# Last graph convolution: weights applied before the aggregation, adjacency blocks as TensorE's stationary operand

## What is computed

```python
def _gcn_conv(x, W, b, src, dst, norm, n_nodes):
    h = x @ W
    msg = h[src] * norm[:, None]
    out = jax.ops.segment_sum(msg, dst, num_segments=n_nodes)
    return out + b
...
    layers = [(W0, b0, a0, g0, beta0), (W1, b1, a1, g1, beta1), (W2, b2, a2, g2, beta2)]
    h = x
    for W, b, a, g, beta in layers:
        c = _gcn_conv(h, W, b, src, dst, norm, n_nodes)
        c = c * jax.nn.sigmoid(a)
        c = _layernorm(c, g, beta)
        h = jax.nn.elu(c)
    return _gcn_conv(h, W3, b3, src, dst, norm, n_nodes)
```

## Time and profile before

| | us |
|---|---|
| median of 3 runs | 3733.86 |
| lowest and highest run | 3727.67, 3737.41 |
| the profiled execution's own time | 3700.42 |
| its span in the trace | 3698.7 |
| four graph convolutions, from the first product to the last pair stored, about | 595 |
| layer 3 of them, from the last weights of layer 2 to the last VectorE operation | 159 |

### The profile page before, as it was taken

How to read it: one execution, slowest core, us unless ns; L and a number is a source line. 1 busy time by engine, 2 the same in 40 slices (tenths; PEclk the granted TensorE clock), 3 DMA queues, 4 the chain that set the end, 5 groups by cost and what they waited for, 6 DMA issues and landing times.

```text
span 3698.7 us, 82678 instructions
## 1 busy us (share of the span) xinstructions
PE 2784.9 (75%) x25480; PEld 1786.5 (48%) x25481; DVE 2202.9 (60%) x7982; ACT 1375.2 (37%) x3073; POOL 1211.2 (33%) x1250
## 2 busy tenths in 40 slices
PE   3211666667689999958888888788888878888887
PEld 1110333333355565535555556555555555555555
DVE  6666888888664534325555555455555555555555
ACT  0322777777632222023333332333333333333332
POOL 1002000000000000015555554455555545555554
PEclk9555888888899999979999999899999989999999
DMA  0002000001111101154444444444444444444443
GB/s 23 0 8 58 37 35 35 35 35 37 58 43 30 56 17 49 56 154 124 121 122 123 127 122 114 118 122 128 121 122 122 121 119 122 124 124 125 122 122 85
DMA packets 197029, 315.97 MB, mean 85 GB/s; under 512 B 36705, under 2 KB 131276, under 8 KB 196924
## 3 DMA queue, kind: packets, MB, share of 16 engines
q1 hardware_dynamic: 155932, 226.92, 20.8%
q0 software_dynamic: 40992, 87.70, 8.4%
HBM read 269.54 MB, written 44.95 MB: 85 GB/s over the span
## 4 chain that ended last, share of the span: by engine, by line
PE 23%; issue 12%; DMA 11%; DVE 4%; another core or an unknown queue 3%; POOL 2%; DVEq 1%; ACT 1%; POOLq 0%; SPq 0%; ACTq 0%
DMA arena<-pair,arena 11%; PE psum L1939 8%; PE psum L1952 6%; PE psum L1963 4%; PE psum L1916 3%; POOL arena L1856 2%; DVE arena L2128 2%; PE psum L1929 1%; DVE arena L2124 1%; DVE arena L2134 1%; DVE arena L2164 1%; PE psum L1890 1%; DVEq L2157 0%; DVEq L2164 0%
## 5 line engine op out<-in xcount | busy, mean ns | idle before, releaser
L1856 POOL DMA_INDIRECT arena<-pair,arena x1212 | 1159.3, 956 | 910.3 <-issue 335.2
L2134 DVE SCALAR_TENSOR_TENSOR arena<-psum,arena,work 128x304 f32<-128x304 f32 x606 | 313.2, 518 | 766.7 <-DMA h<-h 564.0
L1952 PE MATMUL psum<-arena 128*128 128x304 f16 x3939 | 580.0, 294 | 49.2 <-issue 46.4
L2067 ACT ACTIVATE arena<-psum 128x1024 f16<-128x1024 f32 x303 | 310.2, 1024 | 780.8 <-DMA h<-h 311.8
L1939 PE MATMUL psum<-arena 128*128 128x304 f16 x2424 | 380.4, 297 | 182.6 <-DMA arena<-pair,arena 159.2
L1092 PE MATMUL psum<-arena,h 128*128 128x512 f16 x1750 | 481.8, 381 | 19.9 <-DMA h<-h 19.9
L2128 DVE TENSOR_SCALAR arena<-arena 128x304 f16<-128x304 f16 x2121 | 487.1, 300 | 0.0
L1952 PEld LDWEIGHTS psum<-arena 128*128 128x128 f16 x3939 | 360.6, 98 | 242.1 <-issue 129.6
L1963 PE MATMUL psum<-arena 128*128 128x152 f32 (+1 forms) x2496 | 383.6, 299 | 25.7 <-DVE arena L2134 24.5
L1093 PE MATMUL psum<-arena,h 128*128 128x128 f16 x1750 | 384.7, 220 | 0.0
L1916 PE MATMUL psum<-arena 128*32 128x256 f16 x7272 | 328.5, 279 | 63.6 <-issue 57.6
(11 more groups left out here) (258 smaller groups left out, 3430.2 us busy)
## 6 DMA issues: line engine op xcount, KB each, us to landing
work<-winv SPq DMA_DIRECT2D x303, 304.0 KB
arena<-pull SPq DMA_DIRECT2D x303, 224.0 KB
pull<-rows SPq DMA_DIRECT2D x101, 224.0 KB
arena<-pair,arena POOLq DMA_INDIRECT x1212
h<-work SPq DMA_DIRECT2D x12, 640.0 KB, 3.3
h<-h POOLq DMA_DIRECT2D x12, 640.0 KB, 7.5
pair<-arena SPq DMA_DIRECT2D x12, 256.0 KB
x_pad<-arena SPq DMA_DIRECT2D x1, 1600.0 KB, 7.3
```

What stands on the lines that cost most here:

```text
L1856: e.indirect_dma_start(out=t.msg[:, j, k].rearrange("p h f -> p (h f)"), out_offset=None, in_=d[f"pair_{l}"].rearrange("n h f -> n (h f)") ...
L1952: m = e.matmul(p.psum[:, 1, 0:KEYS], t.smsg[:, j % 2, tile, half, :], t.soh[:, j % 2, tile, :], start=(tile == 0 and half == 0), stop=(til ...
L2067: e.activation(t.smsg[:, q, 0:4].rearrange("p k h f -> p (k h f)"), p.psum[:, GATHER:GATHER + 2, :].rearrange("p b n -> p (b n)"), ACT.Cop ...
L2134: e.scalar_tensor_tensor(t.agg[h % 2][:, :, k % BATCH, :], p.psum[:, k % 2, 0:KEYS].rearrange("p (r w) -> p r w", r=REL), t.back[:, l:l + ...
```

## The change

Layer 2 no longer hands on 256 features but 128: when a group's rows are done (`ex`, before they are split into a pair), TensorE transposes them (`turn`), ScalarE copies the transposes back (`turned`), TensorE multiplies them by `W3` (`weigh_rows`), ScalarE takes the high part out of PSUM (`highs`) and VectorE the low part. This pair, half as wide, is stored as `weighted`. So that it fits float16, `W3` is first scaled by a bound: a matmul of ones with |W3| gives column sums, VectorE takes their largest.

Layer 3 (`post`) aggregates 128 features. Its matmuls (`gathered`) have a 128 x 128 block of the adjacency as the stationary operand and the pair of a source block, 256 columns, as the moving one: 125 for a group, 625 for the layer. The result has nodes on the partitions; VectorE adds the high and the low sums with two passes of 5 operations. PSUM for it is double-buffered. `sums` and `weigh` are gone from layer 3, and VectorE's loop over its groups is unrolled.

```diff
-    fin, fout = (RF if l == 0 else HID), (RF if last else HID)
+    pre, post = fast and l == 2, fast and last
+    fin, fout = (RF if l == 0 or post else HID), (RF if last else HID)
...
+    if pre:
+        ho = work[:, 6 * GN:7 * GN].bitcast(F16).rearrange("p (b h f) -> p b h f", b=GB, h=2)
+        kept = wide[:, 0:BLOCKS * 2 * RF].rearrange("p (b h f) -> p b h f", b=BLOCKS, h=2)[:, (GROUPS - 1) * GB:]
+        w3 = work[:, 7 * GN:7 * GN + 2 * RF].rearrange("p (k o) -> p k o", k=2)
+        abs3 = work[:, 7 * GN + 2 * RF:7 * GN + 4 * RF].rearrange("p (k o) -> p k o", k=2)
+        ones = work[:, 7 * GN + 4 * RF:7 * GN + 5 * RF]
...
-    NV = 4 if last else 6
+    NV = 4 if last else 7 if pre else 6
+    OUTS = [lambda i, b=b: 3584 + b * RF if b < 4 else 3328 if i < GROUPS - 1 else 1536 + 2 * RF for b in range(GB)]
...
+        if pre:
+            e.dma_start(w3, d["W3"].rearrange("(k p) o -> p k o", p=P)).then_inc(s_x, 16)
+        if post:
+            e.sem_inc(s_w, 16)
+        else:
+            e.dma_start(p.wts[:, 0:KH, 0:fout], d[f"W{l}"].rearrange("(k p) o -> p k o", p=P)).then_inc(s_w, 16)
         e.dma_start(brow, d[f"b{l}"].partition_broadcast(P)).then_inc(s_w, 16)
         if not last:
             e.dma_start(gain, d[f"g{l}"].partition_broadcast(P)).then_inc(s_w, 16)
...
+        def turn(i, blocks, at):
+            e.wait_ge(s_vq, i * NV + 7)
+            for n, b in enumerate(blocks):
+                for k in range(2):
+                    m = e.transpose(bank[:, at + n * 256 + k * P:at + n * 256 + k * P + P], ex[:, b, k * P:(k + 1) * P],
+                                    p.ident[:, :])
+            m.then_inc(s_tn, 1)
+        def weigh_rows(i):
+            e.wait_ge(s_tc, i + 4 if i < GROUPS - 1 else GROUPS + 5)
+            for b in range(GB):
+                for k in range(2):
+                    m = e.matmul(bank[:, OUTS[b](i):OUTS[b](i) + RF], ex[:, b, k * P:(k + 1) * P], w3[:, k, :],
+                                 start=(k == 0), stop=(k == 1))
+            m.then_inc(s_hw, 1)
+        def gathered(i, q0, q1):
+            at = i % 2 * 2048
+            whole = q1 - q0 == GROUPS
+            if q0 == 0 and i == 1:
+                e.wait_ge(*before.taken)
+            if q0 == 0 and i > 1:
+                e.wait_ge(s_vq, (i - 2) * NV + 2)
+            if q0 == 0 and not whole:
+                e.wait_ge(s_in[0], 16)
+                for two in range(2):
+                    e.matmul(bank[:, at + two * 512:at + two * 512 + 512], h[:, 0, 0, :], before.none, start=True, stop=False)
+            for q in (q0,) if whole else range(q0, q1):
+                if not whole:
+                    e.wait_ge(*(before.written if q == GROUPS - 1 else (s_in[q], 16)))
+                b0, b1 = (0, BLOCKS) if whole else (q * GB, q * GB + GB)
+                for c in range(GB):
+                    for b in range(b0, b1):
+                        m = e.matmul(bank[:, at + c * 256:at + (c + 1) * 256], adj[:, b, i * GN + c * P:i * GN + (c + 1) * P],
+                                     h[:, b].rearrange("p h f -> p (h f)"),
+                                     start=(b == 0 and (whole or c == 4)),
+                                     stop=(b == BLOCKS - 1 and (whole or c in (1, 3, 4))))
+            if q1 == GROUPS:
+                m.then_inc(s_pr, 1)
+        if pre:
+            product(0, 0, 0, GROUPS - 1)
+            e.wait_ge(s_tc, 3)
+            for k in range(2):
+                m = e.matmul(bank[:, 3584:3584 + RF], ones, abs3[:, k, :], start=(k == 0), stop=(k == 1))
+            m.then_inc(s_hw, 1)
+            product(0, 1, 0, GROUPS - 1)
+            product(0, 0, GROUPS - 1)
+            product(0, 1, GROUPS - 1)
+            product(1, 0)
+            weigh(0)
+            for i in range(1, GROUPS - 1):
+                product(i, 1)
+                product(i + 1, 0, 0, 2)
+                turn(i - 1, range(GB), 2048)
+                product(i + 1, 0, 2, 4)
+                weigh_rows(i - 1)
+                product(i + 1, 0, 4)
+                weigh(i)
+            i = GROUPS - 1
+            product(i, 1, 0, 4)
+            turn(i - 1, range(GB), 2048)
+            product(i, 1, 4)
+            weigh_rows(i - 1)
+            weigh(i)
+            def early_turns():
+                turn(GROUPS - 1, (0, 1), 1536)
+                turn(GROUPS - 1, (2, 3), 3584)
+            def late_turn():
+                e.wait_ge(s_tc, GROUPS + 3)
+                turn(GROUPS - 1, (4,), 1536)
+            done.early_turns, done.late_turn, done.weigh_rows = early_turns, late_turn, lambda: weigh_rows(GROUPS - 1)
+        elif post:
+            gathered(0, 0, GROUPS - 1)
+            gathered(1, 0, 2)
+            before.early_turns()
+            gathered(1, 2, 3)
+            before.late_turn()
+            gathered(1, 3, 4)
+            before.weigh_rows()
+            gathered(0, 4, GROUPS)
+            gathered(1, 4, GROUPS)
+            for i in range(2, GROUPS):
+                gathered(i, 0, GROUPS)
...
+        def turned(i):
+            if i < GROUPS - 1:
+                parts = (ex, 2048, GB, i + 1),
+            else:
+                parts = (ex[:, 0:2], 1536, 2, GROUPS), (ex[:, 2:4], 3584, 2, GROUPS + 1), (ex[:, 4:], 1536, 1, GROUPS + 2)
+            for to, at, n, turns in parts:
+                held(e, s_tn, turns, passed)
+                e.activation(to.rearrange("p b f -> p (b f)"), bank[:, at:at + n * 256], ACT.Copy).then_inc(s_tc, 1)
+        def highs(i):
+            to = kept if i == GROUPS - 1 else ho
+            held(e, s_hw, i + 2, passed)
+            if i < GROUPS - 1:
+                held(e, s_st, i * 16 + 16, passed)
+            e.activation(to[:, 0:4, 0, :], bank[:, 3584:4096].rearrange("p (b f) -> p b f", b=4), ACT.Copy).then_inc(s_hi, 1)
+            e.activation(to[:, 4, 0, :], bank[:, OUTS[4](i):OUTS[4](i) + RF], ACT.Copy).then_inc(s_hi, 1)
...
+        if pre:
+            held(e, s_x, 16, passed)
+            for k in range(2):
+                e.activation(abs3[:, k, :], w3[:, k, :], ACT.Abs).then_inc(s_tc, 1)
+            for k in range(KH):
+                sums(0, k)
+            for i in range(GROUPS):
+                if 0 < i < GROUPS - 1:
+                    turned(i - 1)
+                    highs(i - 1)
+                if i + 1 < GROUPS:
+                    sums(i + 1, 0)
+                group(i, i == GROUPS - 1)
+                if i + 1 == GROUPS - 1:
+                    turned(i)
+                    highs(i)
+                if i + 1 < GROUPS:
+                    sums(i + 1, 1)
+            turned(GROUPS - 1)
+            highs(GROUPS - 1)
...
+        if pre:
+            v.link(e, e.memset(ones, 1.0))
+            e.sem_inc(s_tc)
+        if post:
+            v.link(e, e.tensor_scalar(csig, p.cols[:, 3, :], p.small[:, 5:6], None, ALU.mult))
+        elif last:
             v.link(e, e.tensor_copy(csig, p.cols[:, 3, :]))
         else:
             v.inc(e.tensor_scalar(csig, p.cols[:, 3, :], p.small[:, l:l + 1], None, ALU.mult))
             v.link(e, e.tensor_scalar(brow, brow, p.small[:, l:l + 1], None, ALU.mult))
         e.sem_inc(s_vq)
+        if pre:
+            e.wait_ge(s_hw, 1)
+            v.link(e, e.tensor_reduce(ln[:, 66:67], bank[:, 3584:3584 + RF], AX.X, ALU.max))
+            v.link(e, e.tensor_scalar(ln[:, 66:67], ln[:, 66:67], p.small[:, 4:5], 1.01 * SCALE / F16_TOP, ALU.mult, ALU.mult))
+            v.link(e, e.tensor_scalar(p.small[:, 5:6], ln[:, 66:67], 1e-30, None, ALU.max))
+            v.link(e, e.reciprocal(ln[:, 66:67], p.small[:, 5:6]))
+            v.inc(e.memset(abs3, 0.0))
+            v.link(e, e.tensor_scalar(w3, w3, ln[:, 66:67], None, ALU.mult))
...
+            if post:
+                e.wait_ge(s_pr, i + 1)
+                at = i % 2 * 2048
+                for half in range(2):
+                    for b in range(GB):
+                        v.inc(e.scalar_tensor_tensor(u[:, b, :], bank[:, at + b * 256 + half * P:at + b * 256 + half * P + P],
+                                                     cs[:, b:b + 1], brow if half == 0 else u[:, b, :], ALU.mult, ALU.add))
+                    e.wait_ge(s_v, v.now())
+            else:
+                e.wait_ge(s_wm, i + 2)
+                for b in range(GB):
+                    v.inc(e.scalar_tensor_tensor(u[:, b, :], bank[:, 2048 + b * 256:2048 + b * 256 + fout],
+                                                 cs[:, b:b + 1], brow, ALU.mult, ALU.add))
+                e.wait_ge(s_v, v.now())
...
+                if pre:
+                    e.sem_inc(s_vq)
+                    e.wait_ge(s_hi, i * 2 + 1)
+                    v.inc(e.tensor_tensor(to[:, 0:4, 1, :], bank[:, 3584:4096].rearrange("p (b f) -> p b f", b=4),
+                                          to[:, 0:4, 0, :], ALU.subtract))
+                    e.wait_ge(s_hi, i * 2 + 2)
+                    at = OUTS[4](GROUPS - 1 if in_place else 0)
```

(26 more changed lines are left out.)

58 lines of the change are left out of this document (35 added, 23 removed).

## The result

| | before | after |
|---|---|---|
| median of four runs | 3732.29 us (3727.67 to 3737.41) | 3710.67 us (3708.50 to 3711.47) |
| profiled execution: own time, span | 3700.4, 3698.7 | 3711.47, 3709.8 |
| layers 2 and 3 | 330.57 | 309.20 |

The ratio of the medians is 0.9942, with a 95% interval from 0.9926 to 0.9957: the change takes 21.6 us off, 0.58%. The forecast was 3719, in a range from 3704 to 3733. "Layers 2 and 3" runs from VectorE's start on layer 1's fifth group, 0.28 us behind TensorE's first product of layer 2, to VectorE's first operation of the relational stage (`MEMSET arena`). Since it lies inside one execution, it is the measure I use for the parts; it gained 21.4 us, where my sum was 15.1.

A forecast was written before the change was run, and what follows sets the result against it. Layer 3 was taken as bound by TensorE's columns, with VectorE and the stores setting its spacing after. Terms 36.4 - 9.2 - 43.9 + 1.6 = -15.1 us on 3733.9 gave 3718.8, rounded 3719; range 3704 to 3733.

The forecast's parts named there:

- the case's own: The forecast case's own range for the whole kernel: -10 to -20 us, 3714 to 3724; chance 0.66.
- the transposes: Ten transposes on TensorE per layer 2 group, priced 0.217 us apiece, 2.2 us a group.
- rival A: Layer 2's start wait shorter (3704), or layer 3's groups at TensorE's pace, spacing 13.75 (3711); chance 0.14.
- start of layer 2: TensorE stalls 13.1 us at the bound's matmuls, float32 matmuls add 0.4, lower clock 2.2: +15.7 us.
- two periods, first to third group: Layer 2: transposes and W3 matmuls lengthen each 31.54 us period by 4.4: +8.8 us.
- third to fifth group: Layer 2's end: 67.0 us against 55.1, with waits of 4.6 and 2.4 and 1.7 for the clock: +11.9.
- last group of layer 2 to layer 3's first: From the last `weigh`'s end to layer 3's first group: bias load decides, 34.0 us against 43.2: -9.2.
- four spacings of layer 3: VectorE and the stores set 15.65 us a group, 62.6 against 106.45 in all: -43.9 us.
- last group: In layer 3's last group the second pass of additions adds 1.6 us.
- C: Layer 3's adjacency weight loads not hidden, 0.205 us a matmul, TensorE stays the bound: +24 us (3758); chance 0.07.
- B: TensorE's new small waits in layer 2 and the join lower the clock: gain shrinks to about -7 (3727); chance 0.13.

## Why the prediction was right, and what it mis-sized

The direction, the mechanism of each part and the place of each wait were as forecast; the gain was 6 us larger. With the 1.6 us between the two medians of before, the result lies 8 us below the forecast. That is inside the stated range but outside the case's own, whose gains ran from 10 to 20 us, so one term, the transposes, was mis-sized and the rest is made of small ones. The number, 3710.7, is also the one that rival A gave for layer 3 at TensorE's pace (3711); that is chance, since the spacing was 15.2 and not 13.75. Shifts against before, in us:

| step | forecast | measured |
|---|---|---|
| start of layer 2 | +15.7 | +15.6 |
| two periods, first to third group | +8.8 | +6.8 |
| third to fifth group | +11.9 | +12.0 |
| last group of layer 2 to layer 3's first | -9.2 | -11.3 |
| four spacings of layer 3 | -43.9 | -45.6 |
| last group | +1.6 | +1.1 |
| sum | -15.1 | -21.4 |

**Start of layer 2.** Its terms are close, and two small errors cancel: 12.54 us of wait for 13.1, and 2.6 for the clock where I had 2.2, for the clock stood at 0.50 for 5.3 us and not 4.5 (pairs of products start 0.53 us apart until 1306.5, then 0.27). The undone wait gives 15.2 back.

**The transposes: the term that was mis-sized.** I took 0.217 us from the row of fifteen transposes in the earlier trace rows. In after ten at the upper level take 1.26 us (the row at 1357.59), and the next product starts 1.09 us behind their start: 0.11 a pitch. The doubled ones add 0.11 each. The row was taken at the lower level; a window of before over just these 3.4 us says so, and my price left it out:

```profile
2310.90:2314.30 3.40, 3.40 (x16) 3.40 (x17) 3.12 (x8) 1.93 (x3) 0.00 (x0) 0.50 0.83 234
```

The same rows in after, 1.26 us at the upper level and 2.40 behind the wait of 4.46, show both prices in one kernel. It is 1.1 us a group: 2.2 in the two periods (with 2.0 measured), and 1.1 of the 2.1 that the way into layer 3 was shorter. The Trainium skill has a third price, about 275 ns in a kernel's context ("TensorE: Matmul & The Clock Gate", Part 4, PE-mode transpose), with the remark that the clock doesn't come up for transposes. The price doesn't hold here: they took 110 ns each between products at the upper level. On the clock these rows decide nothing, since ten transposes last 1.1 us and stand between products. The longer row of before, of which the earlier trace rows has the first fifteen, goes on to 25 transposes and stayed at 0.50 for all its 5.4 us: that fits the remark, but a single row doesn't show it. A price from a row has to be read with the clock of that row.

**Third to fifth group.** The sum is right because two errors cancel. The waits came as forecast (4.46 for 4.6, 1.94 for 2.4) and the transposes were cheaper, but the clock fell behind both waits, where I had taken 1.7 us as the middle of 0 to 3.4. The filled waits gave 4.0 back: 1.1 in the transposes, 1.7 in the last `weigh`, 1.2 in what stands between them. That is 0.6 above the upper end.

**Into layer 3.** The bias decides, as forecast (3.58 us of wait, rows above). Besides the transposes, the last wait was 1.76 for 2.1 us, and from VectorE's waking to the group's first operation it was 0.67 for 1.0. The prediction speaks of three fifths of product between the transposes and `weigh_rows`; there are two, and its sum of 27.3 counts two. Measured it is 26.0.

**Layer 3's spacing.** 15.2 us on average for 15.65. The stores take 3.8 us for 4.0, the two passes 2.95 with the wait for `x` behind them at 0.2 to 0.7, for 3.22, and the copies 0.28 for 0.4. What hid the stores before was 29 to 31 us a group on TensorE in three of the four spacings and 17.0 in the other. VectorE and the stores set the spacing now, TensorE waits 1.3 to 1.5 us ahead of each of the last three groups. The prediction also said what would come if the stores were hidden, a spacing of 13.75 and 7.6 us more (rival A); that was wrong, since it is 11.35 and 15.2, for the reason that the two sets of buffers showed. This didn't touch the forecast, but it hid from me that the stores were worth twice as much as the rates said.

**The rivals.** C, weight loads that aren't hidden, would have made it slower. 125 `gathered` matmuls take 13.82 us, the last one 0.27 (the row at 1510.43): 0.109 a pitch, with a load of 98 ns hidden in each (the mean of the 625 loads), where I had taken 0.110. So the rule cited in the prediction doesn't hold for these full-array loads; the Trainium skill, same page, Part 3, The mechanism, has beside it the case of a background weight buffer, which agrees with the pitch. Of B, only its clock at the layer's end came true, and half its price was in my sum already; `weigh(i)` never outlasted its cover, as three periods of 34.92 show. Neither half of A came by itself; the runs with the bound later and with two sets of buffers show what each would have given.

**The profiled execution.** I added the shift to the median of the runs, not to the profiled execution's 3700.4. On that one the changed kernel would have been forecast at 3685, and two single executions would have told of a loss of 11 us.

## What to carry to other kernels

When work leaves the engine that bounds a stage, look at once for the waits that its length has hidden, and for what stands queued behind each new wait; here moving one wait behind work that was ready and giving the stores a second buffer were together worth more than the change itself. For a loop of few rounds count the head start, not only the two rates. And with every price from a row, read the granted clock over just that row.
